# Attention stage: the latent, rotary and per-head projections laid out in fewer 128-column passes

## The reference, cut to what matters

```python
b, t, d = x.shape                      # 1, 2048, 256; H, LAT, RD, HD = 16, 64, 64, 16
ql = x @ Wqd                           # 64 latent columns
q = (ql @ Wqu).reshape(b, t, H, HD).transpose(0, 2, 1, 3)
qr = _apply_rope((ql @ Wqr).reshape(b, t, H, RD).transpose(0, 2, 1, 3), cos, sin)
ckv = x @ Wkvd                         # 64 latent columns
k = (ckv @ Wku).reshape(b, t, H, HD).transpose(0, 2, 1, 3)
v = (ckv @ Wvu).reshape(b, t, H, HD).transpose(0, 2, 1, 3)
kr = _apply_rope((x @ Wkr)[:, None], cos, sin)[:, 0]
scores = (einsum('bhtd,bhsd->bhts', q, k) + einsum('bhtd,bsd->bhts', qr, kr)) * scale
scores = where(causal, scores, -inf)
out = softmax(scores) @ v              # then @ Wo, added to x
```

## Time and profile before

| | us |
|---|---|
| median of 3 runs | 3063.18 (3056.26 to 3066.55) |
| span of the profiled execution | 2911.1 |
| outside the span (median less span) | 152.1 |
| PE busy in the span | 2553.8 |
| DVE busy in the span | 1795.2 |
| attention stage in the span | about 204 to 1132 |

### The profile page before, as it was taken

How to read it: one execution, slowest core, us unless ns; L and a number is a source line. 1 busy time by engine, 2 the same in 40 slices (tenths; PEclk the granted TensorE clock), 3 DMA queues, 4 the chain that set the end, 5 groups by cost and what they waited for, 6 DMA issues and landing times. The chain is left out here.

```text
span 2911.1 us, 42096 instructions
## 1 busy us (share of the span) xinstructions
PE 2553.8 (88%) x14687; PEld 1960.8 (67%) x14687; DVE 1795.2 (62%) x3458; ACT 1474.6 (51%) x2894; POOL 1132.5 (39%) x991
## 2 busy tenths in 40 slices
PE   4967999999999997696989989889868998898798
PEld 4855555555555554585877777677768887776687
DVE  7556774874865862755554897889835444445443
ACT  3435547547457455343225886868644434334232
POOL 2642211211212211362332664636346566657232
PEclk9988999999999997798999999999989999999899
DMA  4241000000000001323010000000032233323200
GB/s 158 84 141 44 16 8 23 17 9 23 18 12 15 15 2 60 96 88 119 30 37 8 1 1 8 1 8 1 8 110 86 82 89 94 92 84 100 89 1 30
DMA packets 70267, 138.64 MB, mean 48 GB/s; under 512 B 16816, under 2 KB 38024, under 8 KB 68912
## 3 DMA queue, kind: packets, MB, share of 16 engines
q0 software_dynamic: 26336, 73.01, 8.4%
q1 hardware_dynamic: 43728, 62.95, 6.5%
HBM read 114.71 MB, written 20.81 MB: 47 GB/s over the span
## 5 line engine op out<-in xcount | busy, mean ns | idle before, releaser
L1437 ACT ACTIVATE PT<-ps 128x512 f32<-128x512 f32 (+3 forms) x640 | 313.2, 534 | 283.8 <-PE ps L1190 147.9
L2288 POOL DMA_INDIRECT KV<-kv_scratch,sidx x384 | 368.6, 960 | 217.5 <-issue 131.6
L1303 DVE TENSOR_REDUCE xn<-ps 128x1 f32<-128x512 f32 (+3 forms) x640 | 342.7, 601 | 62.9 <-PE ps L1167 46.7
L35 PE MATMUL ps<-KIh,qih 128*128 128x512 f32 (+2 forms) x640 | 249.5, 390 | 50.3 <-DVE Isc L1872 40.7
L1932 POOL TENSOR_TENSOR part_sum<-part_sum,rlp 128x1024 f32<-128x1024 f32 (+7 forms) x120 | 210.7, 1755 | 89.3 <-ACT rlp L1758 88.3
L1872 DVE SCALAR_TENSOR_TENSOR Isc<-ps,iw,Isc 128x1024 f32<-128x1024 f32 (+7 forms) x216 | 208.5, 965 | 54.2 <-ACT ps L1782 48.8
L36 PE MATMUL ps<-KIl,qih 128*128 128x512 f32 (+2 forms) x640 | 240.4, 376 | 0.0
L37 PE MATMUL ps<-KIh,qil 128*128 128x512 f32 (+2 forms) x640 | 240.2, 375 | 0.0
L1187 PE MATMUL ps<-qB,KB 128*128 128x512 f32 (+2 forms) x640 | 233.9, 365 | 0.0
L2210 ACT ACTIVATE sP<-sP,snm 128x128 f32<-128x128 f32 (+2 forms) x256 | 110.4, 432 | 232.4 <-DVE snm L2273 229.3
L1782 ACT ACTIVATE ps<-ps,iwa 128x1024 f32<-128x1024 f32 (+7 forms) x240 | 198.1, 858 | 48.0 <-PE ps L37 47.6
(11 more groups left out here) (362 smaller groups left out, 6948.5 us busy)
## 6 DMA issues: line engine op xcount, KB each, us to landing
cs<-in_rope SPq DMA_DIRECT2D x20, 512.0 KB, 4.2
ycomb<-y_rows SPq DMA_DIRECT2D x16, 512.0 KB, 5.0
w1raw<-in_w SPq DMA_DIRECT2D x14, 512.0 KB, 6.5
KV<-kv_scratch,sidx POOLq DMA_INDIRECT x384
xn_rows<-xnr SPq DMA_DIRECT2D x8, 512.0 KB, 4.9
whr<-in_whead SPq DMA_DIRECT2D x16, 256.0 KB, 2.8
w2raw<-in_w SPq DMA_DIRECT2D x14, 256.0 KB, 7.0
wir<-in_wi SPq DMA_DIRECT2D x1, 2176.0 KB, 8.0
```

The source lines that it names most:

```text
L35: pe.matmul(out, lhs[0], rhs[0], start=start, stop=False)
L1303: v.tensor_reduce(mp[:, CT * h + r, k:k + 1], o[:, 0:end], AX_X, ALU.max).then_inc(a_free, 1)
L1437: s.activation(PT[:, rnd % 2, hh, lo:CH], ps[:, ST_BANKS[e % 3], lo:CH], ACT.Exp, scale=SCALE).then_inc(a_exp, 1)
L2288: g.indirect_dma_start(KV[:, BG * (k % RB) + m, :], None, a["kv_scratch"], bass.IndirectOffsetOnAxis(sidx[:, t % 2, at:at + 1], 0)).then_i ...
```

## The change

- Latents: the weights `wp` are loaded without their doubled half (columns `0:LAT` of each of the four), so one pass of 128 columns makes query latent and key/value latent together (partitions 0 to 63 and 64 to 127), and a second the rotary part and its swapped copy. 12 matmuls for a chunk, two banks, and the chunks alternate between two pairs of banks. ACT writes the high parts straight to `QL` and `CK`, DVE subtracts them; `tmpl` is gone.
- Rotary part of the queries: one result instead of two, rotary in partitions 0 to 63 and swapped copy in 64 to 127. DVE multiplies each half in an instruction of its own (`turned`), the second from partitions 64 to 127 into 0 to 63 of `rb`. POOL adds 64 partitions in place of 128.
- Plain columns: an even head's pass makes those of the head and of the next one (its own in partitions 64 to 127, the other's in 0 to 63); odd heads have none. The same holds for the keys: K exists for even heads alone and fills `KA[h]` and `KA[h + 1]`. ACT and DVE take the halves one after the other.
- Head weights are 256 columns wide in place of 512, loaded by three DMAs of 64-column pieces in place of one; a table `cs` is loaded by two DMAs of 64 partitions in place of one of 128. `tmpk` has two slots of two halves in place of four; `tmpq` serves one pair of heads.
- `rows_back` and the moved `spread` only keep the tiles behind them at their places.

```diff
-        PE_US = {"S": 0.96, "A": 1.1, "K": 0.94, "P": 1.41, "X": 0.0, "R": 0.2, "F": 0.9, "G": 1.5}
+        PE_US = {"S": 0.96, "A": 1.1, "K": 0.94, "X": 0.0, "R": 0.2, "F": 0.9, "G": 1.5}
...
             if u % NCH == 0:
-                order = [("K", u, 0, 0), ("K", u, 1, 0)] + order + [("K", u, 2, 0), ("K", u, 3, 0)]
+                order = [("K", u, 0, 0)] + order + [("K", u, 2, 0)]
             elif u % NCH == 1:
-                order += [("K", u - 1, h, 1) for h in range(GH)]
+                order += [("K", u - 1, h, 1) for h in range(0, GH, 2)]
...
+            if step[0] == "P":
+                return 0.94 if step[2] % 2 == 0 else 0.47
...
-            for k_ in range({"K": 2, "P": 3, "M": u_ % NCH + 1, "R": 1, "F": 1, "G": 2}.get(kind_, 0)):
+            for k_ in range({"K": 2, "P": 2 - h_ % 2, "M": u_ % NCH + 1, "R": 1, "F": 1, "G": 2}.get(kind_, 0)):
...
-                for w in range(4):
-                    if c >= 1:
-                        pe.wait_ge(a_pd, 4 * (c - 1) + w + 1)
+                for w in range(2):
+                    if c >= 2:
+                        pe.wait_ge(a_pd, 2 * (c - 2) + w + 1)
...
+                o = ps[:, LAT_BANK + 2 * (c % 2), :]
+                v.wait_ge(a_pt, c + 1)
+                v.tensor_tensor(QL[LAT:P, cols], o[0:LAT], QL[0:LAT, cols].bitcast(F32), ALU.subtract)
+                v.tensor_tensor(CK[0:LAT, cols], o[LAT:P], CK[LAT:P, cols].bitcast(F32), ALU.subtract).then_inc(a_pd, 1)
...
+            def turned(o, at):
+                v.tensor_tensor(rb[0:RD, 0, :], o[0:RD], cs[0:RD, at, :], ALU.mult)
+                return v.tensor_tensor(rb[0:RD, 1, :], o[RD:P], cs[RD:P, at, :], ALU.mult)
...
-                        v.tensor_tensor(KA[h][RD:P, HALF * r + CH * w:HALF * r + CH * (w + 1)], o[RD:P],
-                                        tmpk[RD:P, at % 4, :].bitcast(F32), ALU.add).then_inc(a_free, 1)
+                        v.tensor_tensor(KA[h][RD:P, cols], o[RD:P], tmpk[RD:P, at % 2, 0, :].bitcast(F32), ALU.add)
+                        v.tensor_tensor(KA[h + 1][RD:P, cols], o[0:RD], tmpk[RD:P, at % 2, 1, :].bitcast(F32), ALU.add).then_inc(a_free, 1)
...
-                    for w in range(2):
-                        o = full(kind, u, h, r, w)
-                        v.tensor_tensor(rb[:, w, :], o, cs[:, par, w, :], ALU.mult).then_inc(a_free, 1)
-                    o = full(kind, u, h, r, 2)
-                    v.wait_ge(a_tq, GH * u + h + 1)
-                    v.tensor_tensor(qA[RD:P, par, h, :], o[RD:P], tmpq[RD:P, h % 2, :].bitcast(F32), ALU.add).then_inc(a_free, 1)
+                    turned(full(kind, u, h, r, 0), par).then_inc(a_free, 1)
+                    if h % 2 == 0:
+                        o = full(kind, u, h, r, 1)
+                        v.wait_ge(a_tq, (GH * u + h) // 2 + 1)
+                        v.tensor_tensor(qA[RD:P, par, h, :], o[RD:P], tmpq[RD:P, 0, :].bitcast(F32), ALU.add)
+                        v.tensor_tensor(qA[RD:P, par, h + 1, :], o[0:RD], tmpq[RD:P, 1, :].bitcast(F32), ALU.add).then_inc(a_free, 1)
...
-                    s.activation(tmpq[96:P, h % 2, :], ps[96:P, BANK[kind, u, h, r, 2], :], ACT.Copy, scale=rowm[96:P, :]).then_inc(a_tq, 1)
+                    s.activation(tmpq[96:P, 0, :], o[96:P], ACT.Copy, scale=rowm[96:P, :])
+                    s.activation(tmpq[96:P, 1, :], o[32:RD], ACT.Copy, scale=rowm[32:RD, :]).then_inc(a_tq, 1)
...
-                sp.dma_start(whr[:, h % 2, :], a["whead"][:, GH * g + h, :]).then_inc(a_w[h % 2], 16)
+                sp.dma_start(whr[:, k, 0:P].rearrange("p (s t) -> p s t", s=2), heads[:, at, 0:2, 0:RD]).then_inc(a_w[k], 16)
+                sp.dma_start(whr[:, k, P:P + RD], heads[:, at - k + 1, 2 + k, RD:P]).then_inc(a_w[k], 16)
+                sp.dma_start(whr[:, k, P + RD:2 * P], heads[:, at - k, 2 + k, RD:P]).then_inc(a_w[k], 16)
```

More of the change, by code:

```diff
@@ L1145, in attn_tensor @@
                 if kind == "K":
-                    pe.wait_ge(a_wl, GH * g + h + 1)
+                    pe.wait_ge(a_wl, GH * g + h + 2)
                     for w in range(2):
                         o = take(kind, u, h, r, w)
-                        project(o, h, 3, CK, slice(HALF * r + CH * w, HALF * r + CH * (w + 1))).then_inc(a_full, 1)
+                        project(o, h + 1, 1, CK, slice(HALF * r + CH * w, HALF * r + CH * (w + 1))).then_inc(a_full, 1)
                 elif kind == "P":
                     pe.wait_ge(a_wl, GH * g + h + 1)
-                    for w in range(3):
+                    for w in range(2 - h % 2):
                         o = take(kind, u, h, r, w)
@@ L1331, in attn_scalar @@
             k0 = LNA[n]
[L1332 removed]
+            s.wait_ge(a_c, 112)
             s.copy(wp_h[:], wp_raw[:])
@@ L1338, in head_weights @@
             def head_weights(g, h):
[L1339 removed]
+                s.wait_ge(a_w[h % 2], 48 * (GH // 2 * g + h // 2 + 1))
                 s.copy(whh[:, h, :], whr[:, h % 2, :]).then_inc(a_wh, 1)
             def latents(c):
[L1343 to L1347 removed]
+                cols = slice(CH * c, CH * (c + 1))
+                o = ps[:, LAT_BANK + 2 * (c % 2), :]
+                s.wait_ge(a_pq, 2 * c + 1)
+                s.copy(QL[0:LAT, cols], o[0:LAT])
+                s.copy(CK[LAT:P, cols], o[LAT:P]).then_inc(a_pt, 1)
             def rotary(c):
                 s.wait_ge(a_rr, c + 1)
[L1351 to L1352 removed]
+                s.copy(KB[0:RD, CH * c:CH * (c + 1)], rr[0:RD, c % 2, :]).then_inc(a_rh, 1)
             head_weights(0, 0)
@@ L1397, in attn_scalar @@
                         at = KSLOT[kind, u, h, r] + w
+                        o = ps[:, BANK[kind, u, h, r, w], :]
                         s.wait_ge(a_full, PIECE[kind, u, h, r, w] + 1)
-                        if at >= 4:
-                            before = [step for step in KSLOT if KSLOT[step] == at - w - 4][0]
+                        if at >= 2:
+                            before = [step for step in KSLOT if KSLOT[step] == at - w - 2][0]
                             s.wait_ge(a_free, PIECE[before + (w,)] + 1)
-                        s.activation(tmpk[RD:RD + 32, at % 4, :], ps[RD:RD + 32, BANK[kind, u, h, r, w], :],
-                                     ACT.Copy, scale=rowm[RD:RD + 32, :]).then_inc(a_tk, 1)
+                        s.activation(tmpk[RD:RD + 32, at % 2, 0, :], o[RD:RD + 32], ACT.Copy, scale=rowm[RD:RD + 32, :])
+                        s.activation(tmpk[RD:RD + 32, at % 2, 1, :], o[0:32], ACT.Copy, scale=rowm[0:32, :]).then_inc(a_tk, 1)
                 elif kind == "W":
                     if h == 0:
-                        s.wait_ge(a_full, PIECE["P", NCH * u - 1, GH - 1, 0, 2] + 1)
+                        s.wait_ge(a_full, PIECE["P", NCH * u - 1, GH - 1, 0, 0] + 1)
                     head_weights(u, h)
@@ L1449, in attn_gpsimd @@
             k0 = LNA[n]
-            for t in (tmpl, tmpq, tmpk):
+            for t in (tmpq, tmpk):
                 i = p.memset(t[:].bitcast(F32), 0.0)
```

86 lines of the change are left out of this document (41 added, 45 removed).

## The result

The changed kernel takes 3070.3 us (median of 16 runs) where the kernel before takes 3064.0 on the same chip. The ratio is estimated at 1.0026, with an interval of 1.0016 to 1.0037 (the two medians alone give 1.0021). On two later chips (runs e5 and e17) it was 1.0022 [1.0009, 1.0035] and 1.0016 [1.0003, 1.0029]. It is a small loss of 5 to 9 us, where 40 us of gain were forecast.

What follows compares the result with a forecast made beforehand. PE was taken to bound C and D, DVE most of A and the latents, with B mixed. Gains of 34.3 us in the loop and 6 in the latents made 40: 3063.2 to 3023 us, range 2997 to 3050.

Steps and rivals of the forecast that it cites:

- The latents: Ahead of the attention loop, where DVE sets the pace: halved casts, remainders and head weights gain 6 us (3 to 8).
- rival 3: DVE instructions crossing between partition halves take longer, making the kernel slower: 3089 us if twice as long; chance 0.05.
- The preparation of unit 0: Behind the latents, with DVE on its path: half the waits for ACT gained, 1.3 us lost, so nothing.
- B: Loop unit preparing chunk 2's queries while chunk 1 is attended to, 48.0 us, mixed bound: gains 2.1 (-0.2 to 2.8).
- C: Loop unit preparing chunk 3's queries while chunk 2 is attended to, 63.3 us, PE-paced: gains 2.6 (1.5 to 2.8).
- D: Loop unit preparing chunk 0's queries while chunk 3 is attended to, 65.9 us, PE-paced: gains 4.5 (3.5 to 4.7).
- rival 2: DVE's longer chain and banks held for two instructions take the gain back: 11 to 12 us gained, 3052 us; chance 0.15.
- A: Loop unit preparing chunk 1's queries while chunk 0 is attended to, 36.5 us, 63% on DVE: gains 0.5 (-1.3 to 4.7).
- the condition named last: Forecast wrong altogether if the loop's granted clock falls under 0.95 because PE is idle enough in A; no chance given.
- The forecast's low end for the loop: The least gain summed over the loop's units, given as 13.5 us against 34.3 forecast and 55.3 at the high end.
- 152.1 us outside the span: The runs' median exceeds the profiled span of 2911.1 us by 152.1, which the change was said not to touch.
- Rival 4: Little happens, since another chain stands behind PE's in every unit: 3058 us, within 9 us of before; chance 0.05.

Runs made afterwards that it cites:

- e5: The changed kernel itself, unaltered, run again on a second chip: 1.0022 of before.
- e17: The changed kernel itself, unaltered, run once more on a third chip beside its copy with idle-filling matmuls: 1.0016 of before, 2914.0 us.
- e3: The changed kernel with a P step counted at the old cost of 1.41 us in blend, so only the order of steps changes: 0.9979 of before.
- e1: The kernel before, unchanged, profiled once more on another chip to compare stage by stage: 2907.9 us.
- e9: The changed kernel with 96 idle-filling matmuls, never read, ahead of M steps where PE waits (the fill): 0.9991 of before.
- e11: The changed kernel with P counted at 1.41, each head making its own plain query columns and its own keys: 0.9958 of before.
- e6: The kernel before with the changed kernel's costs in blend, so only the order changes and no matmul goes: 1.0033 of before.
- e8: The changed kernel with P counted at 1.41 and each head making its own plain query columns, keys still shared: 0.9979 of before.
- e15: The changed kernel with P counted at 1.41 and each head making its own keys, plain query columns still shared: 0.9976 of before.
- e16: The changed kernel with a P step counted at 1.9 us in blend, dearer than the old 1.41: 1.0031 of before.

## Why the prediction failed, step by step

- **The latents (6 us): right.** 5.2 us, and 5.7 in e3. DVE's pairs start 0.69 to 0.73 apart (0.72 was forecast), the crossing instruction takes 0.68, and POOL's addition 1272 ns. So rival 3 (the crossing costs more) is refuted. By the Trainium skill's rule on two Vector instructions with no wait between them (VectorE: DVE Perf Modes, the section of that name), the trace agrees again: these neighbours begin at different partitions, and none starts before the one ahead of it has ended.

```profile
248.51 0.69 DVE L1243 TENSOR_TENSOR rb<-ps,cs 64x512 f32<-64x512 f32 x1
249.24 0.69 DVE L1248 TENSOR_TENSOR KB<-rr,KB 64x512 fp32r<-64x512 f32 x1
249.96 0.68 DVE L1234 TENSOR_TENSOR QL<-ps,QL 64x512 fp32r<-64x512 f32 x1
250.65 0.69 DVE L1235 TENSOR_TENSOR CK<-ps,CK 64x512 fp32r<-64x512 f32 x1
```

- **The preparation of unit 0 (nothing): wrong by 2.1 to 2.6 us.** From the first matmul of the values to its transposition it takes 40.8 us in place of 38.7 (38.2 in e1), and 40.7 in e3 and 40.4 in e9, so neither order nor the fill explains it; in e11, with nothing shared, it is 39.5. What makes it is open.

- **B, C and D (2.1, 2.6 and 4.5 a unit): the steps that failed.** B went by "PE's 2.8 less what DVE takes back", and C and D alike by PE's share. That rests on the tacit step that a removed matmul leaves every other wait as it was. PE's M steps waited 25.4 us in the loop for the pairs' additions and for qB, in place of 1.4 (their weight loads, at the same places, 34.8 in place of 6.8). One sentence of the prediction says why I believed it: "`blend` puts 4 us between P and H and the next P comes after H". It fails twice. Those 4 us are a sum of the planner's costs, and the diff changed these costs, which I named as code and never priced as an order. And the H behind which the next P comes is head 0's, while head 2's product waits for POOL to add head 1's: DVE's waits for POOL rose from 1.2 to 11.1 us. This second wait is no matter of the order (11.1 in e3 too, 3.2 in e6); it halves, to 5.4, in e8, where each head has its qA addition between the products again. Some of the lines:

```profile
PEld ps L1173 <- ACT qB L1440: 22.2, 25, 2.2
...
PE ps L1173 <- DVE qA L1310: 18.0, 12, 2.1
...
PEld ps L1173 <- DVE qA L1310: 12.6, 8, 2.4
...
DVE rb L1242 <- POOL rr L1483: 11.1, 8, 1.4
```

 And "banks held for two instructions each" stood in rival 2 as an argument, with no wait of PE's worked out for it; it is 2.07 us in one step.

- **C was otherwise sized rightly.** With the old order it is 60.9 (forecast 60.7). The order's share is 63.4 less 60.9, 2.5 us, and the clock's 1.3.

- **D: wrong in size.** 2.1 us in place of 4.5 (1.7 on the mean of the three), and no kernel here has D under 63.5 on the mean. Its first 29.2 us, up to the first projection, are the same in most D units of before, the changed kernel, e3, e6 and e8: nothing is prepared in them. Its 4.7 us could only come from the rest, where the exponentials wait behind the pair's activations. I had put this at 0.2 us for a unit; in the changed kernel PE waits 3.5 us in a D for exponentials (1.26, 1.59 to 1.61 and 0.62).

- **A: 0.5 forecast, 0.7 lost** on a chip like before's (37.2 against 36.5); filled, it is 35.8. That DVE bounds it was right, and it is the clock that hid the gain.

- **The clock: the condition named last was the nearest to what came.** The forecast was to be wrong altogether "if the granted clock in the loop falls under 0.95, because PE has become idle enough in A": it is 0.953 to 0.961, just over that line, and 0.91 in A. I gave it no chance, no price and no place in the range. The row behind it (1.00 with PE 92% busy in A) says nothing of a PE busy 83%, and the forecast itself had A's busy share fall under 85%. That B would have nearly as much half clock as A, behind one wait of 2 us, I did not think of at all.

- **The sum.** On chips of one kind the loop is 7.9 us longer (794.5 against 786.6) where 34.3 less was forecast, 42 us apart. The clock is 12.4 of them (the fill gives them back). Of the 30 left, by the filled kernel's units against the forecast's: C 2.7 a unit, 11 in all; B 2.1, 8; D 3.0, 9. For C the order is the shown cause. For D it is the shared activations and ACT's pace: shown in e3's order, by e15 and e11, and only read from the waits in the changed kernel's own. In B the order gives about 1.0 of the 2.1 (48.0 filled, 47.0 in e3), and the rest is open. The forecast's low end for the loop was also added up wrongly: by its own terms it is 10.5, not 13.5, which is no part of the miss.

- **Span and median.** "152.1 us outside the span" was wrong: the time is 1.8 us over the span in e1. It didn't change the difference, but the likeliest reading of such a gap is two chips.

- **The rivals.** Rival 4 (another chain stands behind PE's in every unit, 3058) named the mechanism nearest to what came, with a chance of 0.05, and stopped at 3058. Rival 2 (0.15) had the held banks, and still a gain of 11 us. A wait that PE's own work had covered, and half clock behind it, is the rival that was missing.

## What to carry to other kernels

If a planner orders the work by costs, an edit of a cost is an edit of the order: price it by itself, by giving the new costs to the old kernel. Matmuls removed from an engine that waits for the result chain of another engine can turn into idle time (55 us of them went here, and idle time rose by 40), and waits of 1 to 2 us can cost a second time in clock (12 us here): read the granted clock where the engine's busy share falls, and try work that computes nothing in the wait before taking the gain as lost. Where a pass is shared by two consumers, what it saves on the one engine can be given back, as here, if its bank, or the engine that takes it out, is held twice as long at a stretch.

## What the hardware showed

96 matmuls that nobody reads made a kernel 11.6 us faster on the same chip (2914.0 to 2902.4), since the granted clock in its loop rose from 0.96 to 0.99. In the changed kernel's loop PE had been busy for 1.9 to 3.6 of the 5 us before each fall to 1.2 GHz, and no idle stretch in the whole loop was over 2.1 us. A fall lasted 3.4 or 6.8 us there (up to 10.2 in e3, e5 and e16). The Trainium skill (TensorE: Matmul & The Clock Gate, section A second HAM failure mode: psum-queue depth-cycling) tells of a kernel in which TensorE idles briefly and often between groups of matmuls, so that its clock goes to and fro between the two levels; this trace agrees, with the waits of 1 to 2 us above.

Chips differed by some 140 us in one stage of the program (gathers at 603 to 611 us, or 743 to 754), while the ratios of the changed kernel on them agree within their intervals.
